# One stage for time mix and projections, and first loads of the heads stage issued inside it

## The reference, cut to what matters

```python
xn = _layernorm(x)
# branch 1: time mix, then channel mix
xln = _ln(_ln(xn, ln1_g, ln1_b), tm_g, tm_b)
mix = xln * time_first + _shift(xln) * (1.0 - time_first)
r = sigmoid(mix @ Wr)
vmix = einsum('bth,th->bh', xln @ Wv, dec)[:, None, :]
x2 = xn + r * (vmix @ Wo + bo)
xc = _ln(_ln(x2, ln2_g, ln2_b), cm_g, cm_b)
out1 = x2 + sigmoid(xc @ Wcr) * (square(relu(_shift(xc) @ Wck)) @ Wcv)
# branch 2: attention, then experts
xa = _rmsnorm(xn, w_ln1)
q, k, v = xa @ Wq.T, xa @ Wk.T, xa @ Wv.T
h = softmax(causal(q k^T * scale)) v
y = xn + h @ Wo.T
out2 = y + moe(_rmsnorm(y, w_ln2))     # 8 experts, top 2
result = x + out1 + out2
```

## Time and profile before

| | us |
|---|---|
| median of 3 runs | 1926.33 (1916.52 to 1930.53) |
| profiled execution | 1919.03 |
| its span | 1917.0 |
| time mix, to the end of its last matmuls | about 257 |
| first instruction of the projections | 261.10 |
| last matmul of the projections | ends about 422 |
| first instruction of the heads stage | 433.83 |

### The profile page before, as it was taken

The page is one execution under the profiler, slowest core; times in us unless marked ns, Lnnn a source line. Parts: engine busy times, 40 slices in busy tenths (PEclk is TensorE's granted clock), DMA queues, the critical chain, the costliest instruction groups (busy, mean ns, idle before and its releaser), DMA issues. The chain is left out here.

```text
span 1917.0 us, 26936 instructions
## 1 busy us (share of the span) xinstructions
PE 1684.8 (88%) x9206; PEld 1432.2 (75%) x9206; DVE 1154.5 (60%) x2173; ACT 1035.3 (54%) x1810; POOL 539.8 (28%) x679
## 2 busy tenths in 40 slices
PE   2888759985999999989999885899999999999997
PEld 2666548864777777777777764789898989898996
DVE  6677522215677767667767463566657575657562
ACT  5455343412566666666666441565656565656562
POOL 3344210000112221221121235333424344433332
PEclk9899979998999999999999998899999999999998
DMA  5455347988336443474445333567768686868672
GB/s 197 116 163 172 98 176 194 238 221 247 89 108 184 119 122 113 112 206 118 123 114 162 90 93 84 213 235 239 243 231 268 209 273 204 277 195 280 213 243 44
DMA packets 114694, 336.72 MB, mean 176 GB/s; under 512 B 29215, under 2 KB 29215, under 8 KB 100338
## 3 DMA queue, kind: packets, MB, share of 16 engines
q1 hardware_dynamic: 93266, 295.86, 47.4%
q0 software_dynamic: 16752, 31.29, 9.3%
q10 hardware_dynamic: 4592, 8.52, 1.2%
HBM read 264.37 MB, written 77.41 MB: 178 GB/s over the span
## 5 line engine op out<-in xcount | busy, mean ns | idle before, releaser
L2086 DVE TENSOR_TENSOR ex_w_lo<-ex_stage,ex_w_hi 128x1024 fp32r<-128x1024 f32 x207 | 249.0, 1237 | 166.9 <-ACT ex_w_hi L1998 158.9
L1230 POOL TENSOR_SCALAR_AFFINE_SELECT hd_p_full<-hd_p_full 128x128 f32<-128x128 f32 (+1 forms) x192 | 95.5, 520 | 448.8 <-ACT hd_p_full L1367 448.5
L1926 POOL TENSOR_TENSOR ex_a_lo<-ex_a,ex_a_hi 128x256 fp32r<-128x256 f32 x128 | 92.5, 746 | 289.1 <-ACT ex_a_hi L2020 288.9
L52 PE MATMUL bank<-ex_x_hi_a,ex_w_hi 128*128 128x256 f32 x512 | 146.7, 287 | 4.9 <-DVE ex_x_lo_a L2103 4.4
L53 PE MATMUL bank<-ex_x_lo_a,ex_w_hi 128*128 128x256 f32 x512 | 145.8, 285 | 0.0
L54 PE MATMUL bank<-ex_x_hi_a,ex_w_lo 128*128 128x256 f32 x512 | 145.8, 285 | 0.0
L52 PE MATMUL bank<-ex_x_hi_b,ex_w_hi 128*128 128x256 f32 x512 | 145.3, 284 | 0.0
L54 PE MATMUL bank<-ex_x_hi_b,ex_w_lo 128*128 128x256 f32 x512 | 144.9, 283 | 0.0
L53 PE MATMUL bank<-ex_x_lo_b,ex_w_hi 128*128 128x256 f32 x512 | 144.9, 283 | 0.0
L1995 ACT ACTIVATE ex_w_hi<-ex_stage 128x1024 fp32r<-128x1024 f32 x134 | 133.8, 1048 | 1.6 <-DMA ex_stage<-in_w_moe 1.6
L52 PE MATMUL bank<-hd_x_hi,hd_up_hi 128*128 128x512 f32 x256 | 105.5, 412 | 27.1 <-DVE hd_a L1457 21.4
(11 more groups left out here) (316 smaller groups left out, 5060.6 us busy)
## 6 DMA issues: line engine op xcount, KB each, us to landing
ex_stage<-in_w_moe SPq DMA_DIRECT2D x69, 1536.0 KB, 7.2
first_w<-in_w_moe SPq DMA_DIRECT2D x23, 1536.0 KB, 7.3
hd_qk<-scratch_qk SPq DMA_DIRECT2D x64, 384.0 KB, 4.2
hd_raw<-in_w_up SPq DMA_DIRECT2D x64, 256.0 KB, 2.8
hd_raw<-in_w_dn SPq DMA_DIRECT2D x64, 256.0 KB, 2.7
scratch_qk<-pj_q_hi SPq DMA_DIRECT2D x32, 256.0 KB, 4.9
scratch_qk<-pj_k_hi SPq DMA_DIRECT2D x32, 256.0 KB, 4.6
tm_x_in<-in_x SPq DMA_DIRECT2D x4, 1024.0 KB, 5.7
```

The costliest lines, as they stand in the source:

```text
L52: pe.matmul(out, lhsT=w_hi, rhs=x_hi, start=first, stop=False)
L1230: pool.affine_select(out=p_full[:, i % 2, at:at + blocks * P], in_=p_full[:, i % 2, at:at + blocks * P], compare_op=ALU.is_ge, fill=0.0, b ...
L1926: pool.tensor_tensor(a_lo[:, chunk.par, m, :], a[:, m, :], a_hi[:, chunk.par, m, :].bitcast(F32), ALU.subtract).then_inc(wide_lo_ready, 1)
L2086: return dve.tensor_tensor(dst, src, hi.bitcast(F32), ALU.subtract)
```

## The change

The two stages become one, `mix_project_phase`. All tiles are declared in one list in which those of the projections lie over time-mix tiles that are done by then, with the waits that this needs. From the time row of the last sequence on, PE, ACT, DVE, POOL and SP get one order that mixes the end of the time mix and the start of the projections. The barrier between them, the second load of the vectors and one load of ACT's function table go. q(0) uses banks 0 to 3, the others 4 to 7.

q and k halves are stored once (64 rows instead of 96 for each part: 4 transfers for each half instead of 8 or 4), and a slot is filled by three transfers: 64 rows, and twice 32 rows for the third group. v is stored by tile of 128 tokens, four transfers of 256 KB.

A class `Streams` holds the slots, the slice buffers and the halves of xc from before the barrier to the heads stage. Slots 0 to 3, slices 0 to 5 and the halves of xc of sequence 0 are loaded during the projections of sequences 1 and 2. The heads stage begins at slot 4 and slice 6.

```diff
+            def features_out(src, which, g, b, out):
+                for part in range(HC):
+                    sp.dma_start(d["qk"][b, part, g * HD:(g + 1) * HD, :, which, :],
+                                 src[part * HD:(part + 1) * HD, :, :].bitcast(F32)).then_inc(out, 16)
+
+            def q_rows_out(b):
+                sp.wait_ge(q_hi_ready, b * HC + HC)
+                features_out(q_hi, 0, 0, b, q_hi_out)
+                sp.wait_ge(q_lo_ready, b * HC + HC)
+                features_out(q_lo, 0, 1, b, q_lo_out)
...
+            def v_rows_out(b):
+                for j in range(TT):
+                    sp.wait_ge(v_ready, b * TT + j + 1)
+                    sp.dma_start(d["v"][b][:, j, :], v_rows[:, j, :]).then_inc(v_out, 16)
+
+            sp.wait_ge(xn_out, 16 * B)
+            sp.wait_ge(stat[A], B * STATS_A)
+            sp.wait_ge(x_turned, B * HC)
+            for n in (0, 2, 1):
+                sp.dma_start(wp_stage[:, n, :], d["w_at"][n]).then_inc(wp_in[n], 16)
+            sp.wait_ge(mix_step, B * HC)
+            sp.wait_ge(x_lo_ready, B * HC)
+            load_xs(0)
             sequence(B - 1, True, False, False)
+            sp.wait_ge(xs_turned, HC)
+            load_xs(1)
+            q_rows_out(0)
             xc_halves_out(B - 1)
+            v_rows_out(0)
+            k_rows_out(0)
+            for b in range(1, B):
+                if b + 1 < B:
+                    sp.wait_ge(xs_turned, b * HC + HC)
+                    load_xs(b + 1)
+                if b == 1:
+                    for done in (q_hi_out, q_lo_out, k_hi_out, k_lo_out):
+                        sp.wait_ge(done, 16 * HC)
+                    sp.wait_ge(xc_out, 32 * (B + 1))
+                    sp.wait_ge(rc_out, 16 * (B + TT))
+                    sp.wait_ge(stat[C], B * STATS_C)
+                    sp.wait_ge(xc_turned, B * HC)
+                    for n in range(3):
+                        sp.wait_ge(wp_lo_ready[n], 1)
+                q_rows_out(b)
+                if b == 1:
+                    streams.load_slot(sp, 0)
+                    streams.load_early_slice(sp, 0)
+                    streams.load_early_slice(sp, 1)
+                k_rows_out(b)
+                if b == 1:
+                    streams.load_slot(sp, 1)
+                    streams.load_early_slice(sp, 2)
+                    streams.load_early_slice(sp, 3)
+                if b == 2:
+                    streams.load_mix(sp, 0)
+                v_rows_out(b)
+                if b == 2:
+                    streams.load_slot(sp, 2)
+                    streams.load_slot(sp, 3)
+                    streams.load_early_slice(sp, 4)
+                    streams.load_early_slice(sp, 5)
+            for done in (q_hi_out, q_lo_out, k_hi_out, k_lo_out, v_out):
+                sp.wait_ge(done, 16 * HC * B)
...
+            norm_x2(B - 2)
+            squares(0)
+            gate_r(B - 1, True)
+            scaled(0)
+            split_xc(B - 2, xcT)
+            act.wait_ge(v_done, B * HC)
+            high_wp(0)
+            high_xp(0)
+            gate_rc(B - 2, xcT)
             norm_x2(B - 1)
+            act.wait_ge(r_done, B * R)
+            act.wait_ge(vmix_step, B * (HC + 1))
+            high_wp(2)
+            high_q(0)
+            squares(1)
             split_xc(B - 1, mix)
+            act.wait_ge(rc_out, 16 * B)
+            copy_v(0)
+            scaled(1)
+            high_wp(1)
             gate_rc(B - 1, mix, True)
+            high_xp(1)
+            high_k(0)
...
+            low_wp(0)
+            low_xp(0)
             dve.wait_ge(xc_turned, (B - 1) * HC)
             norm_x2(B - 1)
             scales(C, B * STATS_C, (B - 1) * 2 + 1)
+            low_wp(2)
+            low_q(0)
+            mean(1)
+            low_wp(1)
+            low_xp(1)
+            low_k(0)
...
+            def turn_xs(b):
+                pe.wait_ge(xs_ready, b * TT + TT)
+                for c in range(HC):
+                    if b == 0:
+                        pe.wait_ge(x2_step, (B - 1) * 2 * TT + TT)
+                    elif b == 1:
+                        pe.wait_ge(rc_ready, B * TT + c + 1)
+                    else:
+                        pe.wait_ge(q_lo_ready, (b - 1) * HC + c + 1)
+                    for j in range(TT):
+                        i = pe.transpose(psum[(HC if b else 0) + c][:, j * P:(j + 1) * P], xs[:, j, c * P:(c + 1) * P], ident)
+                    i.then_inc(xs_turned, 1)
+
+            def by_feature(n, b, bank, free, done):
+                pe.wait_ge(wp_lo_ready[n], 1)
+                for m in range(HC):
+                    if free:
+                        pe.wait_ge(free[0], free[1] + m + 1)
+                    for k in range(HC):
+                        cols = slice(m * P, (m + 1) * P)
+                        last = mm3(pe, psum[bank + m][:, :], wp_hi[n][:, k, cols], wp_lo[n][:, k, cols],
+                                   xp_hi[b % 2][:, k, :], xp_lo[b % 2][:, k, :], k == 0, k == HC - 1)
+                    last.then_inc(done, 1)
...
+            v(B - 1)
+            pe.wait_ge(rc_ready, (B - 1) * TT)
+            r(B - 1)
+            time_row(B - 1)
+            pe.wait_ge(r_ready, B * TT)
+            turn_xc(B - 2)
+            turn_xs(0)
+            rc(B - 2)
+            q(0)
             pe.wait_ge(rc_ready, B * TT)
             turn_xc(B - 1)
+            v_tokens(0)
             rc(B - 1)
+            turn_xs(1)
+            k(0)
+            for b in range(1, B):
+                q(b)
+                k(b)
+                if b + 1 < B:
+                    turn_xs(b + 1)
+                v_tokens(b)
...
+    def load_slot(self, sp, g):
+        b, c, part = self.feature_rows(g)
+        slot, stored = g % self.SLOTS, self.d["qk"][b, part]
+        for rows, which, source in ((slice(0, 2 * HD), slice(0, 2), stored[:, c]),
+                                    (slice(2 * HD, 3 * HD), 0, stored[0:HD, c, 0]),
+                                    (slice(2 * HD, 3 * HD), 1, stored[HD:2 * HD, c, 1])):
+            sp.dma_start(self.qk[rows, slot, which, :].bitcast(F32), source).then_inc(self.slot_in[slot], 16)
+
+    def load_mix(self, sp, b):
+        for dst, name in ((self.x_hi, "xc_hi"), (self.x_lo, "xc_lo")):
+            sp.dma_start(dst[:, :, 2:S + 2].bitcast(F32), self.d[name][b]).then_inc(self.x_in, 16)
...
-            load_slice(0)
-            load_slot(0)
-            load_slice(1)
-            load_mix(0)
-            load_slice(2)
-            load_slice(3)
-            load_slot(1)
-            load_slice(4)
-            load_slice(5)
             for w in range(DEEP):
                 sp.wait_ge(w_lo_ready, w + 1)
                 load_slice(w + RAW)
-                load_slot(w + 2)
+                streams.load_slot(sp, w + streams.EARLY_SLOTS)
             sp.dma_start(vecs[:, :, :], d["vecs"]).then_inc(const_in, 16)
             sp.dma_start(wr[:, :, :], d["w_r"]).then_inc(const_in, 16)
-            for g in range(DEEP + 2, SLOTS):
-                load_slot(g)
...
-                features_out(q_hi, 0, (0, 1), b, q_hi_out)
-                sp.wait_ge(q_lo_ready, b * HC + HC)
-                features_out(q_lo, 0, (2,), b, q_lo_out)
-                sp.wait_ge(k_hi_ready, b * HC + HC)
-                features_out(k_hi, 1, (0, 2), b, k_hi_out)
-                sp.wait_ge(k_lo_ready, b * HC + HC)
-                features_out(k_lo, 1, (1,), b, k_lo_out)
-                sp.wait_ge(v_ready, b * TT + TT)
-                sp.dma_start(d["v"][b], v[:, :, :]).then_inc(v_out, 16)
...
-                        ("qk", [B, HC, 3 * HD, HC, 2, S]), ("v", [B, P, TT, H])):
+                        ("qk", [B, HC, 2 * HD, HC, 2, S]), ("v", [B, P, TT, H])):
...
         constants(nc, ident, causal, d)
-        time_mix_phase(nc, psum, ident[:, :], d)
-        project_phase(nc, psum, ident[:, :], d)
-        heads_phase(nc, psum, ident[:, :], causal[:, :], routing, first_tile, route, d)
+        mix_project_phase(nc, psum, ident[:, :], streams, d)
+        heads_phase(nc, psum, ident[:, :], causal[:, :], routing, first_tile, route, streams, d)
```

517 lines of the change are left out of this document (249 added, 268 removed).

## The result

| | before | after |
|---|---|---|
| median, us (4 runs each, run together) | 1926.24 (1916.52 to 1930.53) | 1871.59 (1869.53 to 1874.55) |
| ratio | | 0.973 (0.971 to 0.975) |
| profiled execution's span, us | 1917.0 | 1867.8 |

The change makes the kernel 2.7% faster; 1871.6 lies in the predicted range and 4 us from the predicted 1876. The gain is 54.6 us between the medians, 49.2 between the two profiled executions. The second number is the one that the traces can take apart.

The account below looks back on a forecast made before the run. PE, busy 88% of the span, was taken to bound the kernel, losing time in waits and at its lower clock. Gains of 34.3 + 7.4 + 5.7 = 47.4 us against the mean 1923.1 gave 1876 us, range 1861 to 1897.

Parts of the forecast that it names:

- before the seam: The first 170 us, ahead of the merged end of time mix and projections: order and waits kept, no gain.
- term 1: Merged end of time mix and projections: next-stage work fills PE's waits, v(3) ends at 387.8 instead of 422.1; gain 34.3 us.
- term 2: Barrier before the heads stage: SP free earlier, v stored by tile, only the last 256 KB behind the end; gain 7.4 us.
- term 3: Start of the heads stage: early loads bring the first channel-mix piece at 6.4 instead of 12.1 us; gain 5.7 us.
- The margins: Merged stretch: 3 us in hand at the turning of xc(3), 2.8 us at its halves.
- my unit: Projections on PE: a block of 48 matmuls takes 11.2 us at 2.4 GHz.
- The edit that I costed at nothing: Stores of q and k: a third less stored, 8 MB in all, given no price since PE did not wait for stores.
- A slipping seam: Merged stretch: late inputs or ACT exceed thin margins, clock falls; 20 us less gain, 1896 us; chance 0.14.
- pacing by slot loads: SP's queue in the heads loop: three issues per slot delay slices, 130 us on the path, 2006 us; chance 0.04.
- 30 us given back: Heads stage: starts with less in flight, first steps wait; 30 us or more back, 1910 us; chance 0.07.
- The range's lower end: 1861 us, from the rival of 10 us more gain (1866 us, chance 0.10) with the runs' scatter of 7 us.

Follow-up runs that it names:

- v_in_one_store: The changed kernel with the values of a sequence stored by one 1 MB transfer instead of four of 256 KB; ratio 0.9731 to the kernel before.

## Why the prediction was right

| step | forecast, us | measured, us |
|---|---|---|
| before the seam | 0 | 2.9 |
| term 1, turning of xc(2) to the end of v(3) | 34.3 | 37.7 |
| term 2, end of v(3) to the heads stage | 7.4 | 6.2 |
| term 3, its start | 5.7 | 6.5 |
| heads stage | 0 | -4.9 |
| experts stage | 0 | 0.8 |
| sum | 47.4 | 49.2 |

The waits and their places were foreseen; that the sum comes within 1.8 us is partly luck. The 3.8 us of faster matmuls and the 2.9 us before the seam were not foreseen, and the heads stage gave 4.9 back.

**Term 1** was right in mechanism and place: 0.76 + 4.88 us of waits ahead of turn_xs(0) and rc(2), 2.2 of lower clock in rc(2) (q(0) starts 13.4 us after it, a block takes 11.2), 1.88 at turn_xs(2); forecast were 0.65, 4.0, 2.3 and 1.4. The last one came out near by luck: the load of xs(2) was issued 4 us earlier than I had it, and took 8.8 us to land behind the stores. The margins held: no wait at the turning of xc(3), none at rc(3), none at turn_xs(1), where I had 1.0. What exceeds the forecast is the block of 48 matmuls, 10.9 us instead of the 11.2 of my unit, 12 x 0.32 = 3.8 us: a duration that I took as fixed while the change moved the tiles. The same is most of the 2.9 us ahead of the seam, where I had written that the first 170 us stay. I had also exchanged two engines' shares: in the first two stretches DVE is busy 37% and ACT 45%; nothing hangs on it.

**Term 2** was mis-sized by 1.2 us, and half wrong in its reason. The order came as forecast: SP had issued the last store of k(3) at 378.9 us, 2.6 us before the last copy, and the last tile of v went out at 382.17, as its copy ended. What failed is the landing "2.0 us against 6.5 for 1 MB". Both figures were taken for a matter of size; with the stores of k and the other tiles still under way the last tile took 3.3 us, and one store of 1 MB with nothing else under way 3.9. So the tiles give 0.6 us, where I had 4.5. The rest of the gain is the shorter queue, 16 stores for 24: before, v was issued 4.0 us after its last copy had ended and took 6.6 us to land. The edit that I costed at nothing carries this term; without it 16 to 18 us of the whole gain are lost.

**Term 3** was mis-sized by 0.8 us: 12.1 us became 5.6 to the first piece, not 6.4. The scores started at 4.6 us, as forecast; they took 1.0 us and the piece joined on. The forecast's own two numbers, 4.6 and 1.2, add up to 5.8 and not to 6.4.

**The rivals.** A slipping seam, pacing by slot loads and 30 us given back did not happen: none of PE's waits over 0.2 us in the changed heads stage ends with a transfer. 4.9 us were given back in the trace, by clock falls that vary from execution to execution. The forecast of 1876 us was 4.4 us too high. The gain between the medians, 54.6 us, is 7.2 more than the 47.4 of the sum, mostly because the profiled execution of before lay 7.3 us below its median and that of after only 2.1 below its own; and I had subtracted from the mean, 1923.1, which lies 3.1 below the median. These two offset each other in part. The range's lower end was added up wrongly too, since 1866 less 7 is 1859 and not 1861; it made no difference.

## What to carry to other kernels

When a stage ends in turnings and splits that wait for each other, put the first products of the next stage between them: here 17 us of waits went that way, and by the traces about as much with the barrier. Before loads are moved ahead into a stage, look at the DMA share there: here it was 0.91 before, and with the early loads and as many stores it rose to 0.95 and the last stores were issued 11 us behind the last copy. Something had to be taken out of the queue first. A trace whose total differs from the median by some us is a sum with a random part: compare events, and count the matmuls at the lower clock, before a mechanism is made of the difference.

## What the runs showed of the hardware

- The start-to-start time of 128x512 matmuls in 4-byte halves, weights loaded anew for each, depends on the base addresses of weights and moving tile: 226.7 ns where they are equal modulo 256, 229 where the moving tile lies 64 bytes higher, 233.3 at the other differences tried (32, 128, and 64 the other way). Addresses at multiples of 64 are not needed (96 and 96 gave 226.7), nor near halves (49 KB apart gave 226.7). The Trainium skill, page "SBUF — State Buffer", section "Who interferes with whom", lists the read of the moving operand and that of the weights as independent; as I read it the addresses should not matter, and the rows say that they do, by 3%. Why slices that start 4 bytes past equal bases gain nearly nothing was not tried further.
- How long a store takes to land was a matter of what was under way. 1 MB took 6.6 us right behind the stores of k(3) in the kernel before and 3.9 us at the same place in v_in_one_store, where the last store of k had landed 0.2 us before its issue; with loads and stores behind it, in the same kernel, 6.1 and 8.5 us. 256 KB took 2.0 us alone (ACT's queue, at the first barrier of the kernel before) and 3.3 us as the last tile of v(3).
- SP's issue of a strided store of 256 KB has a median of 0.60 us for k_hi and 1.12 us for k_lo, which follows it in the same queue (columns: ns min/median/max, first and last start). The four tiles of v(3) behind them took 0.43 to 1.72 us each, one store of 1 MB on a free queue 0.33 us. So here the price of an issue went with what stood in the queue.

```profile
L273 SPq DMA_DIRECT2D scratch_qk<-pj_k_hi x16: 548/604/1461, 278.6 to 373.3; - x16
L273 SPq DMA_DIRECT2D scratch_qk<-pj_k_lo x16: 757/1115/1163, 281.9 to 377.8; - x16
```
